# Sampling terms built from PSUM offsets, the near term on GpSimd, and the window loads cut by column group

## What is computed

```python
xproj  = x @ inproj_w + inproj_b                       # the values that are sampled
x1     = gelu(layernorm(dwconv3x3(x)))
offset = x1 @ off_w + off_b                            # per pixel: 8 groups x 9 points x (x, y)
m      = softmax((x1 @ mask_w + mask_b).reshape(B, H, W, G, P), -1)     # G = 8, P = 9
loc    = ref + dil_grid + offset / norm                # where each point samples xproj
out    = (bilinear_sample(xproj, loc) * m).sum(-1)     # per group of 8 channels
return out @ outproj_w + outproj_b
```

## Time and profile before

| | |
|---|---|
| median of 3 runs | 100.92 us (100.84 to 101.96) |
| the profiled execution, its own time | 101.25 us |
| its span, first to last instruction | 99.6 us |
| PE busy | 88.9 us (89%) |
| DVE busy | 60.5 us (61%) |
| ACT busy | 48.0 us (48%) |
| POOL busy | 24.3 us (24%) |

### The profile page before, as it was taken

How to read it: one execution, slowest core, us unless ns; L and a number is a source line. 1 busy time by engine, 2 the same in 40 slices (tenths; PEclk the granted TensorE clock), 3 DMA queues, 4 the chain that set the end, 5 groups by cost and what they waited for, 6 DMA issues and landing times.

```text
span 99.6 us, 2868 instructions
## 1 busy us (share of the span) xinstructions
PE 88.9 (89%) x1212; PEld 59.9 (60%) x1212; DVE 60.5 (61%) x145; ACT 48.0 (48%) x106; POOL 24.3 (24%) x37
## 2 busy tenths in 40 slices
PE   4999999999897979998968798898999997799980
PEld 1455667548673959875833475474977785564330
DVE  1259863404189889999704225397830969927870
ACT  0453074469999720013002235769625889785000
POOL 7279997000000002999600000000000000500000
PEclk9999999999999999999999999999999999999999
DMA  1999100000256766500000000000000000000003
GB/s 37 364 399 349 41 0 7 0 7 0 79 143 205 208 161 193 176 13 3 7 0 7 0 0 0 7 0 0 0 0 0 0 7 0 0 0 0 0 0 109
DMA packets 3229, 6.27 MB, mean 63 GB/s; under 512 B 528, under 2 KB 1296, under 8 KB 3216
## 3 DMA queue, kind: packets, MB, share of 16 engines
q1 hardware_dynamic: 2784, 4.67, 15.2%
q10 hardware_dynamic: 432, 1.42, 3.8%
HBM read 5.16 MB, written 0.93 MB: 61 GB/s over the span
## 4 chain that ended last, share of the span: by engine, by line
PE 63%; DVE 19%; ACT 10%; issue 5%; DVEq 0%
PE ps L1130 63%; DVE terms L902 3%; DVE ym L893 2%; ACT prod L758 2%; ACT L689 1%; ACT prod L817 1%; DVE lmax L877 1%; DVE smax L968 1%; DVE lsub L880 1%; ACT prob L724 1%; DVE prod L1002 1%; DVE prod L1006 1%; DVE ln_room L918 1%; ACT samp_t L745 1%; ACT x L692 1%
## 5 line engine op out<-in xcount | busy, mean ns | idle before, releaser
L1130 PE MATMUL ps<-terms,wts 64*128 64x256 f32 (+4 forms) x104 | 17.2, 353 | 2.0 <-DVE terms L902 1.2
L1130 PEld LDWEIGHTS ps<-terms,wts 128*128 128x128 f32 (+1 forms) x104 | 13.8, 189 | 4.6 <-issue 1.7
L563 POOL TENSOR_TENSOR prod<-v_win,o_abs 128x1280 f32<-128x1280 f32 x4 | 9.6, 2427 | 22.2 <-DVE terms L902 22.2
L1130 PE MATMUL ps<-prod,ident 32*32 32x256 f32 (+1 forms) x416 | 10.6, 384 | 1.2 <-issue 1.2
L1130 PE MATMUL ps<-prod,wts 128*64 128x256 f32 (+1 forms) x56 | 10.9, 396 | 0.7 <-DVE terms L955 0.5
L638 POOL TENSOR_TENSOR terms<-terms 128x256 f32<-128x256 f32 x2 | 1.4, 728 | 35.6 <-DVE terms L1018 35.6
L1130 PEld LDWEIGHTS ps<-prod,ident 32*32 32x32 f32 (+1 forms) x416 | 6.9, 103 | 4.3 <-issue 2.5
L1130 PE MATMUL ps<-idle 128*128 128x512 bf16 x24 | 7.7, 463 | 1.3 <-DVE idle L823 1.3
L1130 PEld LDWEIGHTS ps<-prod,wts 128*64 128x64 f32 (+1 forms) x56 | 5.9, 158 | 4.5 <-ACT prod L676 1.3
L927 DVE TENSOR_TENSOR prod<-v_win,ps 128x1280 f32<-128x1280 f32 x6 | 8.5, 1468 | 0.0
L1120 DVE TENSOR_TENSOR prod<-prod,ps 128x512 f32<-128x512 f32 x8 | 5.2, 684 | 1.6 <-PE ps L1130 1.6
(11 more groups left out here) (172 smaller groups left out, 157.8 us busy)
## 6 DMA issues: line engine op xcount, KB each, us to landing
v_win<-v_padded SPq DMA_DIRECT2D x20, 128.0 KB, 2.8
wts<-in_w ACTq DMA_DIRECT2D x1, 984.0 KB, 8.2
wts<-in_w SPq DMA_DIRECT2D x1, 640.0 KB, 8.1
v_padded<-s_v SPq DMA_DIRECT2D x1, 400.0 KB, 7.8
wts<-in_w ACTq DMA_DIRECT2D x1, 280.0 KB, 4.1
x_in<-in_x SPq DMA_DIRECT2D x1, 256.0 KB, 3.2
v_padded<-v_tok SPq DMA_DIRECT2D x4, 64.0 KB, 2.0
out<-res SPq DMA_DIRECT2D x2, 128.0 KB, 1.8
```

The costliest lines, as they stand in the source:

```text
L563: g.tensor_tensor(prod[:, bl, dy, :, :].rearrange("p d (x c) -> p d x c", c=GC), win, weights.unsqueeze(3).broadcast_to([P, K5, XG, GC]), ...
L1130: return nc.tensor.matmul(out_, lhsT, rhs, start=start, stop=stop, skip_group_check=True)
```

## The change

- The offsets are made kind by kind: for each of the y offsets, the mask and the x offsets a run of 8 matmuls of 72 columns, each kind in a PSUM bank of its own and signalled by itself (`off_y_done`, `mask_done`, `off_done`). The biases are written by matmuls of 288 columns, kind by kind, four of them ahead of `values`.
- The mask logits are not copied: DVE's maximum and difference read PSUM.
- The far x hats are no longer made. DVE makes the two far x terms from the x offsets in PSUM in one instruction each: min(offset, 0) x ym and max(offset, 0) x ym. The first has the wrong sign, and PE adds it with a negated identity (`minus_ident`, made once on POOL).
- The near x term moves to POOL (`near_terms`, 864 columns for each bl). ACT makes all near hats, and saves the offsets to `s_pos` for the slow path and for |x offset|.
- DVE's order becomes: softmax 0, ym 0, far term 0 of bl 0, softmax 1, far term 2 of bl 0, ym 1, both far terms of bl 1, then the products. Its two flag comparisons move behind the first product of bl 1.
- PE's order: `window_weights` takes the x cells as 0, 1, 2, and both of its bl come ahead of the flags.
- The windows of values are read by column group: 2 halves x 4 column groups, 8 loads for a bl and 16 in all, each to 16 partitions (every fourth one) with all 5 rows.

The diff, without declarations of semaphores and the slow path:

```diff
-        lg = sb("lg", [P, BL, NPT, XG])
+        past = sb("past", [P, BL, 2 * NPT * XG])
+        minus_ident = sb("minus_ident", [P, P])
...
-        def om_ps(bl):
-
-            return ps[:, bl * QB + 2:bl * QB + 4, :].rearrange("p b (k c) -> p (b k) c", k=2)
-
-        def off_ps(bl):
-            return om_ps(bl)[:, :, 0:2 * NPT * G].rearrange("p x (q g) -> p q x g", g=G)
+        def om_ps(bl, kind):
+
+            return bank(bl, (3, 2, 1)[kind])[:, 0:NPT * XG]
+
+        def off_ps(bl, axis):
+
+            return om_ps(bl, axis)
 
         def msk_ps(bl):
-            return om_ps(bl)[:, :, 2 * NPT * G:OM].rearrange("p x (q g) -> p q x g", g=G)
+
+            return om_ps(bl, 2)
...
-                for dy in range(K5):
-                    for bh in range(BH):
-                        p0, p1_ = half(bh)
-                        rows = bass.AP(v_dram.tensor, v_dram[BL * bh + bl, dy].offset,
-                                       [[VP * C, H], [VW, XQ], [1, VWX * C]])
-                        sp.dma_start(v_win[p0:p1_, bl, dy, :], rows).then_inc(v_windowed[bl], 16)
+                for bh in range(BH):
+                    p0, p1_ = half(bh)
+                    for q_ in range(XQ):
+                        cells = bass.AP(v_dram.tensor, v_dram[BL * bh + bl, 0].offset + q_ * VW,
+                                        [[VP * C, H], [VP * C, K5], [1, VWX * C]])
+                        sp.dma_start(v_win[p0 + q_:p1_:XQ, bl, :, :], cells).then_inc(v_windowed[bl], 16)
...
+            g.tensor_scalar(minus_ident[:, :], w("ident"), -1.0, None, ALU.mult).then_inc(minus_ident_set, 1)
...
-            pool.wait_ge(terms_done, K3 * BL)
+            def near_terms(bl):
+
+                pool.wait_ge(ym_done, bl + 1)
+                pool.wait_ge(near_x_done, bl + 1)
+                g.tensor_tensor(terms[:, bl, 1, :, :], ym[:, bl, :, :],
+                                hat[:, bl, 1, 0, :].unsqueeze(1).broadcast_to([P, K3, NPT * XG]),
+                                ALU.mult).then_inc(near_term_done, 1)
+
+            near_terms(0)
+            near_terms(1)
...
-                act.wait_ge(abs_done, bl + 1)
-                a.activation(s_pos[:, bl, :, :].rearrange("p c n -> p (c n)"), o_abs[:, bl, :], ACT.Relu,
-                             bias=w("minus_one"), accum_out=over_sum[:, bl:bl + 1]).then_inc(over_done, 1)
-
-            def hats(bl):
+                act.wait_ge(abs_done, 2 * bl + 2)
+                a.activation(past[:, bl, :], o_abs[:, bl, :], ACT.Relu, bias=w("minus_one"),
+                             accum_out=over_sum[:, bl:bl + 1]).then_inc(over_done, 1)
+
+            def axis_abs(bl, axis, src):
+                a.activation(o_abs[:, bl, axis * NPT * XG:(axis + 1) * NPT * XG], src, ACT.Abs).then_inc(abs_done, 1)
+
+            def near_hat(bl, axis, abs_, done):
+                act.wait_ge(abs_done, abs_)
+                a.activation(hat[:, bl, 1, axis, :], o_abs[:, bl, axis * NPT * XG:(axis + 1) * NPT * XG], ACT.Identity,
+                             bias=w("one"), scale=-1.0).then_inc(done, 1)
+
+            def save_off(bl, axis):
+                a.activation(s_pos[:, bl, axis, :], off_ps(bl, axis), ACT.Copy).then_inc(off_saved, 1)
+
+            def hats_y(bl):
+                act.wait_ge(off_y_done, bl + 1)
+                axis_abs(bl, 1, off_ps(bl, 1))
+                a.activation(hat[:, bl, 2, 1, :], off_ps(bl, 1), ACT.Relu).then_inc(hats_y_done, 1)
+                a.activation(hat[:, bl, 0, 1, :], off_ps(bl, 1), ACT.Relu, scale=-1.0).then_inc(hats_y_done, 1)
+                near_hat(bl, 1, 2 * bl + 1, hats_y_done)
+
+            def hats_x(bl):
                 act.wait_ge(off_done, bl + 1)
-                a.activation(lg[:, bl, :, :].rearrange("p q (x g) -> p q x g", g=G), msk_ps(bl),
-                             ACT.Copy).then_inc(lg_copied, 1)
-                a.activation(points(o_abs[:, bl, :]), off_ps(bl), ACT.Abs).then_inc(abs_done, 1)
-
-                def far_hats(axis, done):
-
-                    off = off_ps(bl)[:, axis * NPT:(axis + 1) * NPT]
-                    a.activation(points(hat[:, bl, 2, axis, :]), off, ACT.Relu).then_inc(done, 1)
-                    a.activation(points(hat[:, bl, 0, axis, :]), off, ACT.Relu, scale=-1.0).then_inc(done, 1)
-
-                far_hats(1, hats_y_done)
-                if bl:
-
-                    act.wait_ge(abs_done, bl + 1)
-                    a.activation(hat[:, bl, 1, :, :].rearrange("p c n -> p (c n)"), o_abs[:, bl, :], ACT.Identity,
-                                 bias=w("one"), scale=-1.0).then_inc(near_hat[bl], 1)
-                    far_hats(0, hats_done)
-                    over(0)
-                    over(1)
+                save_off(bl, 0)
+                act.wait_ge(off_saved, 2 * bl + 1)
+                axis_abs(bl, 0, s_pos[:, bl, 0, :])
+                near_hat(bl, 0, 2 * bl + 2, near_x_done)
+                save_off(bl, 1)
+
+            def mask_exp(bl):
                 act.wait_ge(lsub_done, bl + 1)
                 a.activation(prob[:, bl, :], lsub[:, bl, :, :].rearrange("p q x -> p (q x)"),
                              ACT.Exp).then_inc(prob_done, 1)
-                if bl == 0:
-                    far_hats(0, hats_done)
...
-            hats(0)
-            hats(1)
+            hats_y(0)
+            mask_exp(0)
+            hats_x(0)
+            hats_y(1)
+            hats_x(1)
+            over(0)
+            over(1)
+            mask_exp(1)
...
-                dve.wait_ge(lg_copied, bl + 1)
-                v.tensor_reduce(lmax[:, bl, :], lg[:, bl, :, :].rearrange("p q x -> p x q"), AX_X,
+                dve.wait_ge(mask_done, bl + 1)
+                v.tensor_reduce(lmax[:, bl, :], msk_ps(bl).rearrange("p (q x) -> p x q", q=NPT), AX_X,
                                 ALU.max).then_inc(lmax_done, 1)
                 dve.wait_ge(lmax_done, bl + 1)
-                v.tensor_tensor(lsub[:, bl, :, :], lg[:, bl, :, :],
+                v.tensor_tensor(lsub[:, bl, :, :], msk_ps(bl).rearrange("p (q x) -> p q x", q=NPT),
                                 lmax[:, bl, :].unsqueeze(1).broadcast_to([P, NPT, XG]),
                                 ALU.subtract).then_inc(lsub_done, 1)
-                if bl == 0:
-                    dve.wait_ge(abs_done, bl + 1)
-                    v.tensor_scalar(hat[:, bl, 1, :, :].rearrange("p c n -> p (c n)"), o_abs[:, bl, :], -1.0, 1.0,
-                                    ALU.mult, ALU.add).then_inc(near_hat[bl], 1)
 
             def masked_hats(bl):
 
-                dve.wait_ge(near_hat[bl], 1)
-                dve.wait_ge(hats_y_done, 2 * bl + 2)
+                dve.wait_ge(hats_y_done, K3 * (bl + 1))
                 dve.wait_ge(prob_done, bl + 1)
                 v.tensor_tensor(ym[:, bl, :, :], hat[:, bl, :, 1, :],
                                 prob[:, bl, :].unsqueeze(1).broadcast_to([P, K3, NPT * XG]),
                                 ALU.mult).then_inc(ym_done, 1)
 
-            def window_terms(bl, jx):
+            def far_terms(bl, jx):
 
                 dve.wait_ge(ym_done, bl + 1)
-                if jx != 1:
-                    dve.wait_ge(hats_done, 2 * bl + 2)
-                v.tensor_tensor(terms[:, bl, jx, :, :], ym[:, bl, :, :],
-                                hat[:, bl, jx, 0, :].unsqueeze(1).broadcast_to([P, K3, NPT * XG]),
-                                ALU.mult).then_inc(terms_done, 1)
+                dve.wait_ge(off_saved, 2 * bl + 1)
+                v.scalar_tensor_tensor(out=terms[:, bl, jx, :, :],
+                                       in0=off_ps(bl, 0).unsqueeze(1).broadcast_to([P, K3, NPT * XG]), scalar=0.0,
+                                       in1=ym[:, bl, :, :], op0=ALU.min if jx == 0 else ALU.max,
+                                       op1=ALU.mult).then_inc(terms_done, 1)
...
-            for bl in range(BL):
-                softmax(bl)
-                masked_hats(bl)
-                for jx in (1, 0, 2):
-                    window_terms(bl, jx)
-            flags(0)
-            flags(1)
+            softmax(0)
+            masked_hats(0)
+            far_terms(0, 0)
+            softmax(1)
+            far_terms(0, 2)
+            masked_hats(1)
+            far_terms(1, 0)
+            far_terms(1, 2)
             for bl in range(BL):
                 for dy in range(K5 - len(POOLED)):
                     products(bl, dy)
+                    if bl and not dy:
+                        flags(0)
+                        flags(1)
...
-            def offset_bias(bl):
-                for i in range(2):
-                    mm(om_ps(bl)[:, 2 * i:2 * i + 2, 0:OM], ones[:, :],
-                       b_row[:, C:C + OM].unsqueeze(1).broadcast_to([PARTS, 2, OM]), True, False)
+            def bias_rows(bl, kinds):
+                for kind in kinds:
+                    rows = b_row[:, C + kind * NPT * G:C + (kind + 1) * NPT * G].rearrange("p (q g) -> p q g", g=G)
```

(41 more changed lines are left out.)

19 lines of the change are left out of this document (10 added, 9 removed).

## The result

The changed kernel takes **103.27 us** (median of 4 runs, 102.47 to 103.78), the kernel before 100.95 in the same session (100.84 to 101.96). The ratio is 1.020, with a 95% interval of 1.011 to 1.029: slower clear of noise, though the interval does not say whether by more or less than 2%, and 0.3 us under the 103.6 that was forecast. The profiled execution took 103.26 us with a span of 101.2; the one of before took 101.25 with 99.6.

What follows compares the result with a forecast made beforehand. PE alone was taken to bound the kernel from 37.36 us to the last slab copy; 1.0 us of late weights plus 1.7 behind the flags added 2.7, giving 103.95 us profiled, 103.6 against the median, range 101.8 to 105.1.

Steps and rivals of the forecast that it cites:

- Offsets by kind: PE's offset matmuls: 24 narrow ones per bl, bound by strided weight loads, take 3.1 us, 1.4 more than now.
- Zeros, weights, no wait for terms: On PE, zeros start at 31.7 us; both windows of weights follow without waits, the second ending at 43.2 instead of 42.2.
- The terms: Sampling terms from DVE and POOL are ready before PE asks; nearest cover 0.8 us for bl 1's first far term.
- Loads: Sixteen value loads by column group instead of twenty bring nothing and cost nothing, landing at most 0.2 us after the weights.
- The flags: DVE's flags behind its fourth product, complete at 44.9 us, leave PE idle from 43.2 to 45.0; 1.7 us counted.
- The sum: Late weights of 1.0 us plus 1.7 us behind the flags make the program 2.7 us longer.
- late weights: PE's second window of weights ends 1.0 us later, after the longer offset runs use up the 0.6 us waits.
- rival B: Window sums run through after PE's wait for the flags, giving back 1.6 to 2.3 us: 101.3 to 102.0 us; 18%.
- rival D: Late loads, idle PE lowering the clock to 1.2 GHz, or another gap inside the sums: 105 to 107 us; 10%.

Runs made afterwards that it cites:

- experiment 3: Changed kernel with x1 written so that each offset matmul's 64 weight columns are contiguous instead of every fourth: 103.56 us, ratio 1.020.
- 5: Changed kernel with contiguous offset weights and DVE's flags ahead of its first product of bl 1: 101.96 us, ratio 1.013.
- 4: Changed kernel with the kernel before's 20 row-by-row loads of values instead of the 16: 103.31 us, ratio 1.019.
- Experiment 1: Changed kernel with DVE's flag comparisons moved ahead of its first product of bl 1: 102.58 us, ratio 1.010.
- Experiment 2: Kernel before with only the flags late: PE's behind both windows of weights, DVE's behind the first product of bl 1: 104.01 us, ratio 1.026.
- 6: Kernel of 5 with ACT's exponential of bl 1 moved to right behind hats_y(1): 100.34 us, ratio 0.990 to the kernel before.
- 8: Kernel before with x1 stored so that its offset matmuls load contiguous weights: 101.78 us, ratio 1.011.
- 12: Kernel before with two more semaphores that nobody uses, one run: 102.18 us with a span of 100.5.
- 11: Changed kernel with near terms on VectorE, between the two far terms of a half, instead of GpSimd: 103.28 us, ratio 1.023.
- 9: Kernel of 6 with 13 matmuls on zeros ahead of the weights instead of 8: 100.83 us, ratio 0.988 to the kernel before.
- 10: Kernel of 9 with PE's flags between the windows of weights and DVE's ahead of all products: 101.15 us, ratio 0.996 to the kernel before.
- Experiment 7: Changed kernel with the exponential of bl 1 early and no matmuls on zeros ahead of the weights: 105.21 us, ratio 1.045.

## Why the prediction was right

**Offsets by kind: 3.1 us forecast, 3.09 and 3.03 measured** (24.50 to 27.59, 27.94 to 30.97). The reason holds too. It rested on the stride of the weights (the row for `values` against the earlier trace rows), and experiment 3 separates the two: same matmuls, contiguous weights, 1.65 us (25.62 to 27.27). Per record that is 63 ns strided and 34 ns contiguous. The Trainium skill (TensorE: Matmul & The Clock Gate, LDWEIGHTS) gives columns / 1.2 ns, 53 ns for 64 columns; neither row agrees.

**Zeros, weights, no wait for terms: confirmed**, with the zeros holding PE for 1.74 us and the two windows 4.74 and 4.84 us (the forecast took 4.92 and 4.91). Seen from the first offset, the second window ends at 17.79 us, forecast 17.9 (43.2 less 25.3).

**The terms: hidden, and the cover was thin, as stated.** The forecast had bl 1's first far term 0.8 us ahead of PE. In the trace it ends at about 36.9 and PE takes it at 37.45. Experiments 3 and 5 show what happens when PE is early: it waits 1.47 us for that term. GpSimd's near term takes 2.03 us (864 columns), within the 1.6 to 2.4 forecast, and is no bound.

**Loads: nothing gained or lost**, confirmed by 4. The last of the sixteen was issued at 36.4 us and they took 4.3 us to land (5.0 at most, against 2.8 and 3.5 for the twenty), so all were there by 41.4, ahead of the weights at 42.3. The forecast had the shorter landing time.

**The flags: 1.7 us forecast; 1.65 us of idle PE measured**, ended by the step named. Experiment 1 takes 1.35 of it away. Measured from the first offset, the weights are 0.82 us late (17.79 against 16.97) and the sums start 1.89 behind them; the forecast had 1.0 and 1.8, of which it counted 1.7.

**The sum: +2.7 forecast, +2.71 measured in the stage.** The attribution of 1.0 us to late weights and 1.7 to the flags is only one way to cut it. Experiment 2 has the late flags without the longer offsets and loses 2.69 as well, and experiment 3 has late flags with short offsets and keeps 19.42. With the flags behind the fourth product, DVE comes to that product 0.38 us ahead of the weights in the changed kernel, so a shorter offset run buys no more than about that: 0.3 us in 3. With the flags early it bought 0.25 (5 against 1), and together with the moved exponential 1.96 (6 against 1). The three edits are worth 1.35 (flags), 0.25 (dense loads) and 1.71 us (exponential) in this order. What the exponential is worth without the other two was not run. So the stage's total was forecast to 0.01 us, but not as a sum of two costs that could each be taken away for its price.

**Two sizes were off, and cancel; that part of the agreement is luck.** The profiled time is 0.69 us under the 103.95 of the forecast: 0.80 less ahead of the offsets and 0.70 less in the sums, 0.39 more behind them and 0.41 more outside the span. The forecast kept 10.78 us for the window sums; they took 0.70 less, under half of what rival B wanted. B's mechanism, the wait ahead of the sums, is not what sets their length: experiments 4 and 5 wait 1.65 and 0.30 us ahead of them and both take 9.43, experiment 6 waits 0.30 and takes 9.39, experiment 1 waits 0.30 and takes 10.25. (Experiment 2, with 2.45 and 11.26, ran in part at the lower clock and can't be compared.) What can be said is where the gaps lie. In the kernel before and in 2, 8 and 12 they come behind record 221 of the run on `prod,ident` and 127 later; in the changed kernel and in 1, 3, 4, 5, 6 and 11 behind record 155; with five more zeros, in 9 and 10, behind 150. A record here is a load and a matmul, so from before to after the place moves by 66 x 2 = 132 instructions. The change puts exactly that many more on PE ahead of it: 32 more offset matmuls of two records (128) and 2 more biases (4). So the gaps are tied to the count of PE's instructions, and the distance of 126 to 128 records makes about 256 instructions from one to the next. At these places start-to-start distances are 0.3 to 1.4 us, against under 0.2 elsewhere in the run at the upper clock level. The second place is the one that made the sums shorter: 0.30 us in the changed kernel (0.58 in 1), and not to be told from its surroundings in 3, 4, 5, 6 and 11, where it was 1.15 before. The Trainium skill (Runtime: NRT & Kernel Launch, Instruction fetch mechanics) gives blocks of 256, with which these rows agree, and says that crossing one is mostly hidden, with which they do not. The third such place now lies behind the sums, a distance of 0.52 us after nine records on copied slabs (0.25 in 1, 3, 4, 5, 6 and 11), and is part of the +0.39 of the table. Experiment 7, with 8 zeros fewer, shows no gap at its place, record 163, which PE reaches at 48.05 us, still at the lower clock. Why one costs 0.3 and another 1.4 stays open; it differs between kernels with the same code there (0.79 and 1.15 in the kernel before, 0.53 and 0.88 in 8, 1.06 and 1.43 in 12).

The second size is the time outside the span, 0.41 us more, which the forecast had at nothing. Every run listed of the kernels with GpSimd's near term shows 2.0 to 2.1 us, every run of the kernel before and of 2, 8 and 12 has 1.63 to 1.73, and with the near term moved to DVE it is 1.8. The flags, the stride of `x1`, the loads and two semaphores are excluded as causes. About 0.3 us goes with the two instructions on GpSimd; the mechanism and the last 0.1 are open. Of the remaining differences, 0.8 us came back ahead of the offsets, 0.1 by the biases moved behind the variances, the rest at the first matmuls on `x_in`, which ran at a clock that had already risen (at 4.6 us, in the kernel before at 6.1). Other kernels with the changed sampling start their offsets at 24.3 to 25.6 (24.3 in 9, where the clock rose at 4.0), so this is scatter of the profiled execution and no part of the change.

**The granted clock fell, in a place where the forecast did not expect it, and it cost nearly nothing.** The page of the changed kernel has

```profile
PEclk9999999999589999999999999999999999999999
```

with 0.50 to 0.56 from 25 to 28 us, the 1.2 GHz level, in the middle of the strided offset runs, with PE busy all the time before. The run of 48 records took 3.09 us there and 3.03 in experiment 4 (25.53 to 28.56), at full clock throughout. So the strided run hardly goes with this clock. It is different with dense loads: 2.94 us at the lower level (experiment 9, 24.26 to 27.20) and 1.66 at the upper one (experiments 5 and 6). What makes the clock fall there is open. In the four profiled executions in which it fell during the offsets (the changed kernel, 1, 9 and 11) it had first risen at 4.0 to 5.9 us; in the kernel before, 2 to 8 and 12 it rose at 6.1 to 7.4 and did not fall there, in 3 to 7 with the same narrow matmuls (strided loads in 4 and 7, dense ones in 3, 5 and 6). The fall that the forecast did name, behind the idle time ahead of the sums (rival D), is absent in the changed kernel, 3 and 4 (1.65 us of idle) and in 11 (2.14), and present in 2 (2.45) and 7 (2.06).
